# A mixture-of-experts kernel: the down product of the 64-slot tile with two operands side by side, and one scatter more

## What is computed

```
idx = argsort(-score, axis=0)[:cap].T            # 32 x 320 tokens
up  = einsum('eci,eji->ecj', xf[idx], w_up);  gate, upv = split(up, 2)
ye  = einsum('ecj,eoj->eco', silu(gate) * upv, w_down)
out = zeros(T, C).at[idx].add(w[..., None] * ye)
```

## Time and profile before

| | |
|---|---|
| median of 3 runs | 2360.45 us (2357.5 to 2361.66) |
| the profiled execution | 2361.54 us, its span 2359.6 us |
| TensorE busy | 1971.2 us (84%) |
| VectorE, ScalarE, GpSimd busy | 1491.6 us (63%), 1331.8 us (56%), 823.7 us (35%) |
| attention, routing, experts, last norm | to about 1485, 1786, 2307, 2360 us |
| 96 scatters (L1426) | 148.2 us, mean 1544 ns |
| 1440 down matmuls (L1463, `y_ps`) | 181.0 us |
| 1920 up matmuls (L1463, `up_ps`) | 288.9 us |
| granted clock over the whole run | 0.922 |

### The profile page before, as it was taken

One profiled execution on the slowest core, in us unless ns is written; L12 is line 12 of the kernel. 1 busy time (PEld: TensorE's weight loads), 2 busy tenths in 40 slices (PEclk: granted clock), 3 DMA queues, 4 the chain that ended last, 5 costly groups with the idle time before them and its releaser, 6 DMA issues. The chain is left out here.

```text
span 2359.6 us, 43734 instructions
## 1 busy us (share of the span) xinstructions
PE 1971.2 (84%) x14340; PEld 1794.1 (76%) x14340; DVE 1491.6 (63%) x3318; ACT 1331.8 (56%) x3381; POOL 823.7 (35%) x937
## 2 busy tenths in 40 slices
PE   5799999999999999999999987501176999999990
PEld 5699988888988888988888876500155999999990
DVE  6655566656566656666666775288864666666655
ACT  4666665666665666665666653200065666666655
POOL 1122333333333333333111110000095666766652
PEclk9999999999999999999999998555598999999995
DMA  1000011001001001000000110300002444454428
GB/s 60 27 10 21 21 30 32 24 28 33 21 30 32 24 28 32 22 30 28 23 26 24 32 32 21 147 0 0 0 0 83 149 143 134 149 167 150 149 52 285
DMA packets 91405, 135.81 MB, mean 58 GB/s; under 512 B 16932, under 2 KB 79376, under 8 KB 87148
## 3 DMA queue, kind: packets, MB, share of 16 engines
q1 hardware_dynamic: 75372, 123.52, 15.2%
q0 software_dynamic: 15872, 10.24, 2.6%
HBM read 104.62 MB, written 39.85 MB: 61 GB/s over the span
## 5 line engine op out<-in xcount | busy, mean ns | idle before, releaser
L474 PE MATMUL out_ps<-v_sb,probs_t 128*128 128x64 f32 x4352 | 551.0, 271 | 17.6 <-DVE attn L773 15.1
L474 PEld LDWEIGHTS out_ps<-v_sb,probs_t 128*128 128x128 f32 x4352 | 532.4, 194 | 27.4 <-DVE probs_t L750 20.6
L736 DVE TENSOR_REDUCE part_max<-scores_ps 128x1 f32<-128x512 f32 (+3 forms) x576 | 356.9, 621 | 205.0 <-PE scores_ps L439 148.8
L611 ACT ACTIVATE probs<-scores_ps,neg_max 128x512 f32<-128x512 f32 (+3 forms) x640 | 398.1, 627 | 45.0 <-DVE neg_max L740 42.7
L439 PE MATMUL scores_ps<-k_st,q_parts 128*128 128x512 f32 (+3 forms) x1280 | 410.8, 403 | 11.4 <-ACT probs L611 5.0
L456 PE MATMUL probs_t_ps<-ident,probs 128*128 128x128 f32 x2176 | 347.6, 275 | 1.0 <-DVE probs_t L750 1.0
L620 ACT COPY probs_t<-probs_t_ps 128x512 f32<-128x512 f32 (+3 forms) x416 | 208.5, 501 | 244.6 <-PE probs_t_ps L456 243.2
L456 PEld LDWEIGHTS probs_t_ps<-ident,probs 128*128 128x128 f32 x2176 | 261.4, 142 | 51.4 <-issue 2.6
L1463 PE MATMUL up_ps<-xe_t,w 128*128 128x320 f32 x1920 | 288.9, 310 | 2.4 <-DVE xe_t L1570 1.7
L1463 PEld LDWEIGHTS up_ps<-xe_t,w 128*128 128x128 f32 x1920 | 283.6, 189 | 3.0 <-issue 1.9
L439 PEld LDWEIGHTS scores_ps<-k_st,q_parts 128*128 128x128 f32 x1280 | 200.5, 193 | 25.2 <-ACT probs L611 7.2
(11 more groups left out here) (214 smaller groups left out, 3153.8 us busy)
## 6 DMA issues: line engine op xcount, KB each, us to landing
w_raw<-in_w_expert SPq DMA_DIRECT2D x32, 1536.0 KB, 6.4
w_raw<-in_w_adapter SPq DMA_DIRECT2D x32, 384.0 KB, 6.9
x_t<-in_x_t SPq DMA_DIRECT2D x64, 128.0 KB, 2.1
x_row<-in_x SPq DMA_DIRECT2D x64, 128.0 KB, 2.0
x_rows<-x SPq DMA_DIRECT2D x64, 128.0 KB, 1.7
acc_rows<-x SPq DMA_DIRECT2D x64, 128.0 KB, 1.8
ln_x<-acc_rows SPq DMA_DIRECT2D x16, 512.0 KB, 6.2
out_rows_dram<-ln_y SPq DMA_DIRECT2D x16, 512.0 KB, 5.2
```

The lines of the kernel that those rows point to most:

```text
L474: mm = pe.matmul(o_ps[:, h, :], probs_t[:, g % PT_RING, a - lo:a - lo + P], v_sb[:, slot(b, a // P), h, :], start=a == 0, stop=a == t * P)
L611: act.activation(probs[:, g % PROBS_RING, 0:hi - lo], s_ps[:, g % AHEAD, 0:hi - lo], ACT.Exp, bias=neg_max[:, u % 8:u % 8 + 1], accum_out= ...
L736: red = dve.tensor_reduce(neg_max[:, ring:ring + 1] if single else part_max[:, ring, c:c + 1], s_ps[:, g % AHEAD, 0:hi - lo], AX.X, ALU.ma ...
```

## The change

The third tile has only 64 slots, so its 128-column stationary slice was half empty. Now the other 64 columns of `h_parts[:, 0, p, 256:384]` hold the remainder of the same slots. One matmul with both halves and the upper weights gives upper x upper in partitions 0 to 63 and remainder x upper in 64 to 127 of PSUM; a second, with only the upper 64 columns and the remainder weights, adds to partitions 0 to 63. That is two matmuls a chunk instead of three. The two halves aren't added on the chip's engines: both are evicted and scattered to the same tokens, the second in a fourth indirect DMA. It starts when the third has completed, and `SCATTERS` = 4 takes the place of `SL` in all counts of `scattered`. The eviction of the upper partitions needs the weights there too, so the routing block copies the third tile's weights to the other 64 partitions through a DMA from SBUF to SBUF. VectorE makes the remainders of `h` in two instructions (256 and 64 columns), and its memset of the unused columns is gone.

```diff
@@ route
+            sp.wait_ge(slots_listed, 1)
+            sp.dma_start(twin_weight[P // 2:P, :], twin_weight[0:P // 2, :]).then_inc(twinned, 16)
...
             dve.tensor_copy(slot_weight[:].rearrange("p a b -> p (a b)"), ps[0][:, COLS:2 * COLS])
             dve.drain()
+            dve.tensor_copy(twin_weight[:], slot_weight[:, :, SL - 1]).then_inc(slots_listed, 1)
             dve.scalar_tensor_tensor(tok_f[:], ps[0][:, 0:COLS], -1.0, empty[:], ALU.add, ALU.add)
             dve.drain()
             dve.tensor_copy(slot_token[:].rearrange("p a b -> p (a b)"), tok_f[:])
+            dve.drain()
+            dve.wait_ge(twinned, 16)
+            dve.tensor_copy(slot_weight[P // 2:P, :, SL - 1], twin_weight[P // 2:P])
@@ experts, GpSimd
-                    wait(pool, scattered, 16 * SL * (e - 1), pool_passed)
+                    wait(pool, scattered, 16 * SCATTERS * (e - 1), pool_passed)
...
-                wait(pool, scattered, 16 * SL * e, pool_passed)
-                for t, n in enumerate(slots):
-                    wait(pool, out_ready, SL * e + t + 1, pool_passed)
+                wait(pool, scattered, 16 * SCATTERS * e, pool_passed)
+                parts = [(t, 0, n) for t, n in enumerate(slots)] + [(LAST, HALF, P)]
+                for t, lo, hi in parts:
+                    if lo:
+                        wait(pool, scattered, 16 * (SCATTERS * e + SL), pool_passed)
+                    else:
+                        wait(pool, out_ready, SL * e + t + 1, pool_passed)
                     pool.indirect_dma_start(
-                        out=dram["acc"], out_offset=bass.IndirectOffsetOnAxis(ap=token[0:n, r, t:t + 1], axis=0),
-                        in_=out[0:n, r, t, :], in_offset=None, bounds_check=T - 1, oob_is_err=False,
+                        out=dram["acc"], out_offset=bass.IndirectOffsetOnAxis(ap=token[0:hi - lo, r, t:t + 1], axis=0),
+                        in_=out[lo:hi, r, t, :], in_offset=None, bounds_check=T - 1, oob_is_err=False,
                         compute_op=ALU.add).then_inc(scattered, 16)
@@ experts, TensorE, down
+                    if t == LAST:
+                        both, upper = h_parts[:, 0, p, t * P:(t + 1) * P], h_parts[:, 0, p, t * P:t * P + HALF]
+                        if p:
+                            pe.matmul(y_ps[0:HALF, t % 2, 0:D], upper, w[:, r, 1, col:col + D], start=False, stop=False)
+                        mm = pe.matmul(y_ps[:, t % 2, 0:D], both, w[:, r, 0, col:col + D],
+                                       start=p == 0, stop=p == PAIRS - 1)
+                        if not p:
+                            mm = pe.matmul(y_ps[0:HALF, t % 2, 0:D], upper, w[:, r, 1, col:col + D], start=False, stop=False)
+                        return mm
@@ experts, ScalarE
-                    act.activation(out[0:n, r, t, :], y_ps[0:n, t % 2, 0:D], ACT.Copy,
-                                   scale=weight[0:n, r, t:t + 1]).then_inc(out_ready, 1)
+                    act.activation(out[:, r, t, :], y_ps[:, t % 2, 0:D], ACT.Copy,
+                                   scale=weight[:, r, t:t + 1]).then_inc(out_ready, 1)
@@ experts, VectorE
-            dve.memset(raw(h_parts[:, :, :, cap:]), 0.0)
...
-                    dve.tensor_tensor(h_parts[:, 1, p, 0:cap], h[:, ring_p], raw(h_parts[:, 0, p, 0:cap]),
-                                      ALU.subtract).then_inc(h_split, 1)
+                    full = LAST * P
+                    dve.tensor_tensor(h_parts[:, 1, p, 0:full], h[:, ring_p, 0:full], raw(h_parts[:, 0, p, 0:full]),
+                                      ALU.subtract)
+                    dve.tensor_tensor(h_parts[:, 0, p, cap:cap + HALF], h[:, ring_p, full:cap],
+                                      raw(h_parts[:, 0, p, full:cap]), ALU.subtract).then_inc(h_split, 1)
```

More of the change, by code:

```diff
@@ L976, in route @@
         empty = sb("empty", [P, COLS])
+        twin_weight = sb("twin_weight", [P, E])
         tok_f = sb("tok_f", [P, COLS])
@@ L986, in route @@
         col_ready, listed = sem("col_ready"), sem("listed")
+        slots_listed, twinned = sem("slots_listed"), sem("twinned")
         LISTED, ODD = 2, LOT // 2 + 1
@@ L1326, in experts @@
     PART = W // PAIRS
-    assert W % PAIRS == 0 and SL >= 2
+    HALF = P // 2
+    LAST = SL - 1
+    SCATTERS = SL + 1
+    assert W % PAIRS == 0 and SL >= 2 and slots[LAST] == HALF
     with ExitStack() as ctx:
@@ L1445, in _ @@
                 body(E - 2 + r, r, first=False, ahead=False)
-            wait(pool, scattered, 16 * SL * E, pool_passed)
+            wait(pool, scattered, 16 * SCATTERS * E, pool_passed)
         @block.tensor
@@ L1550, in body @@
                         if not first:
-                            act.wait_ge(scattered, 16 * SL * (e - 1))
+                            act.wait_ge(scattered, 16 * SCATTERS * (e - 1))
                         act.wait_ge(staged, 2 * e + 2)
-                    act.activation(out[0:n, r, t, :], y_ps[0:n, t % 2, 0:D], ACT.Copy,
-                                   scale=weight[0:n, r, t:t + 1]).then_inc(out_ready, 1)
+                    act.activation(out[:, r, t, :], y_ps[:, t % 2, 0:D], ACT.Copy,
+                                   scale=weight[:, r, t:t + 1]).then_inc(out_ready, 1)
             pairs_of_experts(act, body)
```

## The result

| | before | after |
|---|---|---|
| median | 2361.05 us (2357.5 to 2363.93, 4 runs) | 2415.02 us (2411.22 to 2415.86, 4 runs) |
| ratio | | 1.0226, 95% interval 1.0208 to 1.0244 |
| profiled execution, its span | 2361.54 us, 2359.6 us | 2414.57 us, 2412.7 us |

What follows compares the result with a forecast made beforehand. TensorE's loop (15.38 us an expert) bound the kernel, GpSimd's having 1.26 us to spare. With GpSimd slowest at 16.7 us: 29 steps +38.3, last two -1.2, tail +3.8, routing +2.0, together +42.9 us: 2403 us, range 2383 to 2440.

Steps and rivals of the forecast that it cites:

- TensorE: Tile 2's down matmuls: 15 become 10, saving 0.61 us an expert; loop 14.77 us, shape changes taken as costing nothing.
- Rival (c): Changes of stationary shape stall TensorE 0.17 us each, GpSimd's loop staying below 16.13 us: +29 us, 2389; chance 0.05.
- VectorE: Split of `h_parts` in two instructions: 149 ns fixed each, at most 0.75 us an expert, covered by VectorE's idle time.
- GpSimd's loop: Scatters, gathers and stage copies of an expert, with fourth scatter and wait: 16.7 us, bounds 16.0 to 18.5 us.
- The gap: Ahead of each fourth scatter: 1.6 us to completion plus 0.89 us to start, about 2.4 us (2.0 to 3.0).
- The relief by an idle VectorE: GpSimd's last gather and both stage copies run faster once VectorE is idle: 1.24 us counted of 1.48.
- rival (a): GpSimd gets no relief from an idle VectorE: loop 17.94 us, +78.8 us, 2439; chance 0.22.
- Rival (d): Accumulating writes complete much later than shown: +30 us per further us, 2451 at 1.6 us more; chance 0.05.
- Start: Routing's end: copying `slot_weight` by a small SBUF-to-SBUF DMA delays the barrier by +2.0 us (1.7 to 2.6).
- End: Kernel's tail: the final scatter comes 3.8 us later (3.4 to 4.4), from gap 2.4 plus scatter 1.43.
- Rival (b): TensorE stays the slowest loop and the matmul saving comes through in 31 steps: -13.1 us, 2347; chance 0.04.
- The clock: TensorE's new pauses: if the clock fell there, the up product would be slower and the step longer; no size given.

Runs made afterwards that it cites:

- the padded kernel: The changed kernel with five more matmuls in tile 2 of each expert, adding zeros from a zero moving operand: 2402.73 us, ratio 1.0177.
- the zero rows in the kernel before: The kernel before with a fourth scatter adding 64 rows of zeros after each third, behind the same wait for completion: 2399.06 us, ratio 1.0168.
- `stage` first with the third tile second: The changed kernel with scatters ordered tile 0, tile 2 lower half, tile 1, tile 2 upper half, and stage(e) ahead of the gathers: 2346.47 us, ratio 0.9935.
- `stage` first: The changed kernel with stage(e) ahead of gather(e + 2) in GpSimd's queue: 2359.88 us, ratio 0.9989; the same swap in the kernel before: 2361.03 us, ratio 0.9997.
- the fourth scatter behind a gather: The changed kernel with the fourth scatter issued behind the first gather of the next expert's turn: 2373.12 us, ratio 1.0053.
- the third tile second: The changed kernel with scatters ordered tile 0, tile 2 lower half, tile 1, tile 2 upper half, stage still behind the gathers: 2371.04 us, ratio 1.0047.
- no wait: The changed kernel with the fourth scatter adding to DRAM rows of its own, without waiting; output lacks the remainder's part of tile 2: 2358.64 us, ratio 0.9987.
- without the fourth scatter: The changed kernel without the fourth scatter and its wait; output lacks the remainder's part of tile 2: 2342.49 us, ratio 0.9929.

## Why the prediction was right, and what was off in it

The side, the place and the mechanism were right: GpSimd's queue, with the wait for completion ahead of `stage`, became the slowest loop, and the saved matmuls vanished in TensorE's new idle time. By its steps:

- **TensorE.** Forecast 14.77 us with changes of stationary shape at nothing; 14.75 us when nothing else binds. The matmuls of tile 2 start 0.12 us apart (2043.48, 2043.60, 2043.72 above) with no idle time of PEld between 128 and 64 columns. Rival (c) falls. The drain of the Trainium skill (TensorEngine Tiling (Array Packing), Key Properties) doesn't show at this alternation of columns; whether it is a change of tiling mode at all, no row shows. Before the 64-row transposes the 0.17 us stay.
- **VectorE.** The two subtractions take 418 and 218 ns on average against 486: 150 ns more, the forecast's number. Their cover held.
- **GpSimd's loop.** Forecast 16.70 us, measured 16.88 in the expert shown and 16.99 as a mean of 29; the nearness hides terms that cancel. The gap is 1.91 us, not 2.4: the last scatter's 1.14 us to completion was the better row (1.02 + 0.89), the 1.6 us from packets was too much: -0.49 us in this expert (the view of waits gives a mean of 2.15 us over 20). The gap of 2.9 us that was worked out from the Trainium skill (DMA: Bandwidth & Descriptors, Anatomy of one DMA) was further off. The relief by an idle VectorE is whole: gathers 3.44 us instead of 4.08, copies 0.31 instead of 1.38, 1.71 us where I counted 1.24: -0.47 us. So rival (a) falls, and its premise with it. Between scatter and gather 1.23 us pass instead of 1.43: -0.20. Against that the third scatter takes 2.15 us instead of 1.45 and the fourth 2.04 instead of 1.43: +0.70 and +0.61; with 0.04 us from `stage` to the eviction this makes +0.2. Rival (d) falls too: the longest of these gaps between 1840 and 2280 us was 2.97 us.
- **The term that was off** is "relief" as a one-way effect. I worked out which GpSimd instructions leave VectorE's busy time, and not which come into it: with five matmuls fewer the up product starts sooner after the eviction, VectorE's first subtraction moves onto the start of the third scatter, and 12 us (by the padded kernel) to 16 us (by the zero rows in the kernel before, 1.6 of it from the twin weights) are lost by work saved. It is a mis-sized term of the sum, not another mechanism.
- **Start.** +2.0 forecast, 1.6 measured for the twin weights; the transfer and its release take 1.74 us from issue to the copy (1786.65 to 1788.39), not 2.1.
- **End.** +3.8 forecast, +6.0 measured up to the barrier: the gap and scatter are 3.3 us (1.85 + 1.42), the DRAIN brings 2.7. Last two steps: -1.2 forecast, -1.3 measured.
- **Rival (b)** (TensorE stays the slowest loop, 2347 us) is what `stage` first with the third tile second gives: 2346.5.
- **The clock**, which the prediction left open, did fall in the new pauses: six times, for 3.4 us each, the granted clock was 0.50 (1.2 GHz instead of 2.4), as in the window below, 1874.40 to 1877.80 us. Each time it fell 0.04 to 1.5 us after TensorE had started again behind a pause of 1.86 to 2.48 us; 17 other pauses of 1.86 us or more had no fall behind them. The up product of such an expert takes 10.29 instead of 8.96 us:

```profile
1874.40:1877.80 3.40, 3.40 (x16) 3.40 (x15) 0.00 (x0) 0.47 (x1) 2.97 (x2) 0.50 0.41 149
```

```profile
1873.36 0.39 PE L1506 MATMUL y_ps<-w,h_parts 128*128 128x256 f32 x1 [1.87 <-ACT out_rows L1577]
...
1874.84 10.29 PE L1478 MATMUL up_ps<-xe_t,w 128*128 128x320 f32 x60
```

  It costs nearly nothing here: the next pause shrinks from 1.87 to 0.45 us, and the step grows from 16.88 to 17.00 us, under 1 us in all six. The kernel before, and the kernels above whose pauses stay mostly under 0.9 us (`stage` first, the fourth scatter behind a gather, the third tile second, no wait), show no fall in their 31 steps; the zero rows in the kernel before show six, the padded kernel two, each behind a pause of 1.87 to 1.89 us.
- **Slips in the arithmetic.** 1.6 + 0.89 is 2.49, which the prediction carries as 2.4 (30 times 0.09 is 2.7 us too little); and a loop of 16.0 us is 0.62 us above 15.38, not 0.66, so the low end would be 2382. Neither changes the forecast's side. That the total came within 12 us is partly luck, as the terms of the loop show.

## What to carry to other kernels

An extra dependent DMA is priced by what stands behind it in its engine's queue: here 1.9 us of wait and 1.5 to 2 us of descriptor writing mattered mostly because two small copies, which the output path waits for, stood behind the gathers: with these ahead, 55 of the 70 to 72 us are gone. Put what others wait for first, and put an independent DMA between two dependent ones. And when an edit shortens one engine's part, look not only at which instructions it frees from a collision but at which ones it moves into one.

## What the runs showed of the hardware

- **A scatter that starts inside a VectorE subtraction ends at a fixed time after that one's start.** Between 1840 and 2280 us of after, 21 scatters started 0.10 to 0.13 us after the start of the 768-column subtraction (0.95 us long) and took 2.13 to 2.15 us; one at 0.18 us took 2.08, three at 0.22 to 0.24 us 2.02 to 2.03, one at 0.40 us 1.85, eight at 0.69 to 0.72 us 1.54 to 1.56. Offset and length sum to 2.25 to 2.26 us each time: 1.43 us counted from 0.82 us into the subtraction. In `stage` first (after), 12 third scatters that started 0.84 to 0.90 us into it took 1.43. The 23 third scatters of the padded kernel that start 0.46 to 0.56 us before it take 1.43 to 1.44 us, though it runs beside most of them. So only the start is held up.
- **The edge is sharp.** In the runs without the wait and without the fourth scatter, the 27 third scatters that started 0.01 to 0.04 us after the subtraction took 1.43 to 1.45 us, the 27 that started 0.05 to 0.14 us after it 2.13 to 2.23 us. (Two fourth scatters of the padded kernel, at 0.03 and 0.04 us, took 2.22.) So some 0.05 us more or less decides over 0.7 us, and such a collision can come and go within one execution, as in the run without the wait.
- **What is held up.** By the Trainium skill (SBUF — State Buffer, Who interferes with whom) a VectorE instruction with two SBUF inputs contends with a GpSimd instruction that reads SBUF; the rows agree. The same section infers that the writing of descriptors needs the write side only and so isn't held up by such an instruction; these scatters, up to 0.8 us longer, were.
- **Four more scatters** at 0.69 to 0.71 us took 2.01 to 2.04 us. The one at 2051.59 above ended 1.44 us after the end of VectorE's next subtraction (L1612, 2051.77 to 2052.19). The eight that took 1.54 to 1.56 us stood at the same place to both subtractions, so what decides between the two is open. One of the eight, the first row being the subtraction:

```profile
2067.77 0.95 DVE L1587 TENSOR_TENSOR w<-w_raw,w 128x768 fp32r<-128x768 f32 x1
...
2068.48 1.54 POOL L1441 DMA_INDIRECT acc_rows<-out_rows,token  x1 [1.93 <-DMA acc_rows<-out_rows,token]
```

- **GpSimd's DRAIN at the barrier** took 3741 to 3745 ns with 96 scatters in the program (before, before with `stage` first, and after without the fourth) and 6191 to 6481 ns with 128 (after, the zero rows in the kernel before, and all the others). It began 1.3 us after the end of the last scatter in all of them, also where the third and the last followed each other without the wait. It lies on the path. Why it grows isn't settled.
